# Tables of angles moved beside the projections' batches; columns moved by three engines with a store for each kind

## The reference

```python
q = (x @ Wq).reshape(B, T, H, DK)          # B, T, D = 8, 512, 128; H, DK, M = 8, 64, 8
k = (x @ Wk).reshape(B, T, H, DK)
v = (x @ Wv).reshape(B, T, H, DV)
beta = sigmoid((x @ Wbeta).reshape(B, T, H, M))
tg = sigmoid((x @ Wtg).reshape(B, T, H, M))
angles = pos[:, None, None, None] * omega_scale[None, :, :, None] * inv_freq
cos, sin = jnp.cos(angles), jnp.sin(angles)      # for each time, head, mode and pair: 32 pairs
qr = l2norm(rotary(q, cos, sin)) * scale
kr = l2norm(rotary(k, cos, sin))
g = jnp.log(jnp.clip(tg * rho, 1e-06))
# a scan over time with a state for each mode, batch and head: it takes qr, kr, v, g, beta;
# its outputs are weighted by softmax(mode_logits), gated, multiplied by Wo, and go to the experts
```

## Time and profile before

| | us |
|---|---|
| median of 3 runs | 4490.09 |
| lowest, highest | 4484.92, 4506.94 |
| profiled execution | 4485.37 |
| its span, first to last instruction | 4483.6 |
| project, to the start of tables (15.0 to 276.4) | 261.4 |
| tables with its barrier (276.4 to 391.4) | 115.0 |
| recurrence and experts | 4092.2 |

### The profile page before, as it was taken

How to read it: one execution, slowest core, us unless ns; L and a number is a source line. 1 busy time by engine, 2 the same in 40 slices (tenths; PEclk the granted TensorE clock), 3 DMA queues, 4 the chain that set the end, 5 groups by cost and what they waited for, 6 DMA issues and landing times. The chain is left out here.

```text
span 4483.6 us, 194752 instructions
## 1 busy us (share of the span) xinstructions
PE 3845.0 (86%) x86225; PEld 3102.0 (69%) x86225; DVE 3612.9 (81%) x6975; ACT 2886.8 (64%) x9736; POOL 377.9 (8%) x220
## 2 busy tenths in 40 slices
PE   5511799899999998999899999999998999979999
PEld 2201677777777777777777777777777777756666
DVE  5663988888988888888888888888988888825665
ACT  5752577677766776767677666776766767644443
POOL 1130000000000000000000000000100000000000
PEclk8755899999999999999999999999999999989999
DMA  4667222322232223222322322232223222121110
GB/s 118 173 166 164 60 60 56 91 58 56 56 93 56 63 62 89 60 56 67 82 56 56 80 69 56 56 92 56 56 56 93 56 56 62 50 60 37 34 34 8
DMA packets 319915, 314.47 MB, mean 70 GB/s; under 512 B 139864, under 2 KB 252384, under 8 KB 314976
## 3 DMA queue, kind: packets, MB, share of 16 engines
q1 hardware_dynamic: 319072, 302.00, 26.6%
HBM read 232.70 MB, written 69.21 MB: 67 GB/s over the span
## 5 line engine op out<-in xcount | busy, mean ns | idle before, releaser
L911 DVE TENSOR_TENSOR run_XL<-run_XL,run_EL 128x30 f32<-128x30 f32 (+14 forms) x1920 | 637.6, 332 | 66.0
L910 DVE TENSOR_TENSOR run_EL<-run_AL,run_XL 128x30 f32<-128x30 f32 (+14 forms) x1920 | 637.1, 332 | 66.0
L978 POOL TENSOR_TENSOR run_DB<-run_DB,run_below 128x1024 f32<-128x1024 f32 x128 | 305.0, 2383 | 3310.7 <-DVE run_KP L895 1747.0
L1045 PE MATMUL run_SP<-run_KP 64*32 64x128 f32 x8192 | 552.9, 275 | 30.0 <-DVE run_KP L895 21.7
L871 DVE TENSOR_TENSOR run_SC<-run_SP,run_DB 128x512 f32<-128x512 f32 x512 | 341.2, 686 | 266.9 <-PE run_SP L1049 261.4
L794 ACT ACTIVATE run_DB<-run_DB,run_col 128x64 f32<-128x64 f32 x2048 | 548.0, 351 | 4.7 <-POOL run_DB L978 1.0
L801 ACT ACTIVATE run_KD<-run_PR,run_col 128x64 f32<-128x64 f32 x2048 | 480.3, 328 | 18.4 <-PE run_PR L1064 10.2
L854 ACT COPY run_S<-run_KS 128x256 f32<-128x256 f32 x448 | 166.7, 372 | 504.4 <-PE run_KS L1111 502.4
L1045 PEld LDWEIGHTS run_SP<-run_KP 64*32 64x32 f32 x8192 | 412.6, 107 | 99.2 <-issue 74.2
L807 ACT ACTIVATE run_R<-run_KS,run_col 128x64 f32<-128x64 f32 x1792 | 415.1, 324 | 65.5 <-PE run_KS L1072 65.3
L1007 PE MATMUL run_PR<-ident,run_win 128*64 128x128 f32 x4096 | 285.2, 282 | 169.5 <-DMA run_win<-KQ_s 153.8
(11 more groups left out here) (204 smaller groups left out, 7630.6 us busy)
## 6 DMA issues: line engine op xcount, KB each, us to landing
run_DB<-G_s SPq DMA_DIRECT2D x512, 128.0 KB, 3.0
run_EG<-EG_s SPq DMA_DIRECT2D x128, 512.0 KB, 6.9
run_tab<-TAB_s SPq DMA_DIRECT2D x128, 256.0 KB, 11.8
KQ_s<-proj_win SPq DMA_DIRECT2D x32, 768.0 KB, 7.7
run_win<-KQ_s SPq DMA_DIRECT2D x64, 384.0 KB, 3.2
TAB_s<-tab_tab SPq DMA_DIRECT2D x128, 128.0 KB, 2.4
run_V<-V_s SPq DMA_DIRECT2D x128, 128.0 KB, 3.1
V_s<-proj_vv SPq DMA_DIRECT2D x64, 128.0 KB, 3.2
```

Of the source, the lines that this page charges most:

```text
L910: v.link(dve.tensor_tensor(e, bcast(AL[:, r + 1:, r], 2, done), bcast(XL[:, r, 0:done], 1, rows), ALU.mult))
L911: less = dve.tensor_tensor(XL[:, r + 1:, 0:done], XL[:, r + 1:, 0:done], e, ALU.subtract)
L1045: pe.matmul(out[64 * e:64 * e + C, p].rearrange("p (z u) i -> p z (u i)", z=2), KP[f, key, p, t0:t1], KP[f, kq, p, t0:t0 + SPAN], start=Tr ...
```

## The change

The block `tables` is gone. Its work on a head's tables stands in `project`, head h beside batch h (there are eight of each). On DVE it is cut into four pieces, `angles(b, i)`, one ahead of each tile's sums. On ACT `swing` (the sines) stands at the head of `end(b)`, and `weigh` (the weights) at the next `after(b, 0)`. The buffers `ang` and `turns` are single now. On SP `put_tables(b - 1)` with its 16 stores comes behind the V_s of batch b, and the last head's behind the last KQ_s.

A new block `columns` makes only the 48 copies: ACT the first kind, DVE the second, POOL the third, 16 each, and SP stores each kind when it is there. `cols` has the kind outermost now, so that a store's contiguous piece in DRAM is 32 floats (128 B), where that of the single store was 96 floats (384 B).

```diff
+        ang, turns = sb("ang", [128, 2, T]), sb("turns", [128, 2, T])
+        tab = sb("tab", [128, 2, 4, 2, T])
+        freq = col[:, 1:2]
...
+                def put_tables(h):
+                    sp.wait_ge(tab_done, 3 * (h + 1))
+                    for e in range(2):
+                        for q in range(2):
+                            at = 64 * e + 32 * q
+                            for k in range(4):
+                                sp.dma_start(TAB_s[h, k, e, :, q::2, :], tab[at:at + 32, h % 2, k]).then_inc(put_t[h % 2], 16)
+
                 for b in range(3):
                     load(b)
+                sp.dma_start(pos[:, :], c_pos).then_inc(l_pos, 16)
+                sp.dma_start(col[:, :], c_col).then_inc(l_pos, 16)
...
+                    if b:
+                        put_tables(b - 1)
                 late(B - 1)
+                put_tables(H - 1)
                 for u in range(2):
                     sp.wait_ge(put_x[u], 16 * (B // 2))
                     sp.wait_ge(put_v[u], 16 * 2 * NT * (B // 2))
+                    sp.wait_ge(put_t[u], 16 * 16 * (H // 2))
...
+                def swing(h):
+                    u = h % 2
+                    act.wait_ge(reduced, h + 1)
+                    if h >= 2:
+                        act.wait_ge(put_t[u], 16 * 16 * (h // 2))
+                    act.activation(tab[:, u, 1], ang[:, :], ACT.Sin).then_inc(tab_done, 1)
+                    act.activation(turns[:, :], ang[:, :], ACT.Abs).then_inc(swung, 1)
+                    act.wait_ge(swung, 2 * h + 1)
+                    act.activation(tab[:, u, 0], turns[:, :], ACT.Sin, scale=-1.0, bias=col[:, 0:1]).then_inc(swung, 1)
+
+                def weigh(h):
+                    u = h % 2
+                    act.wait_ge(swung, 2 * h + 2)
+                    act.wait_ge(tab_done, 3 * h + 1)
+                    for j in range(2):
+                        last = act.activation(tab[:, u, 2, j], tab[:, u, 0, j], ACT.Copy, scale=w_part[:, h, j:j + 1])
+                    last.then_inc(tab_done, 1)
+                    for j in range(2):
+                        last = act.activation(tab[:, u, 3, j], tab[:, u, 1, j], ACT.Copy, scale=w_part[:, h, j:j + 1])
+                    last.then_inc(tab_done, 1)
+
                 def after(b, i):
 
+                    if i == 0:
+                        weigh(b)
                     if i == 1:
                         act.wait_ge(decay_in, b + 1)
                         act.activation(z[:, b % 2, :, 0:HM], ez[:, b % 2, :, 0:HM], ACT.Ln).then_inc(logs_out, 1)
@@ -371,6 +416,7 @@
 
                 def end(b):
 
+                    swing(b)
                     if b + 2 < B:
                         act.wait_ge(std_in, b + 3)
                         act.activation(std[:, b % 2], std[:, b % 2], ACT.Sqrt).then_inc(std_out, 1)
...
+                def angles(h, i):
+
+                    a, r = (t[:, :, :].rearrange("p a t -> p (a t)") for t in (ang, turns))
+                    if i == 0:
+                        if h == 0:
+                            dve.wait_ge(l_pos, 32)
+                        else:
+                            dve.wait_ge(swung, 2 * h)
+                            dve.wait_ge(tab_done, 3 * (h - 1) + 1)
+                        for j in range(2):
+                            v(dve.tensor_scalar(ang[:, j], pos[:, :], om_part[:, h, j:j + 1], freq, ALU.mult, ALU.mult))
+                        v.wait()
+                    elif i == 1:
+                        v.link(dve.tensor_scalar(r, a, 1.0 / TWO_PI, ROUND, ALU.mult, ALU.add))
+                        v.link(dve.tensor_scalar(r, r, ROUND, None, ALU.subtract))
+                    elif i == 2:
+                        for part in (CW1, CW2):
+                            v.link(dve.scalar_tensor_tensor(out=a, in0=r, scalar=-part, in1=a, op0=ALU.mult, op1=ALU.add))
+                    else:
+                        v.link(dve.scalar_tensor_tensor(out=a, in0=r, scalar=-CW3, in1=a, op0=ALU.mult, op1=ALU.add))
+                        dve.tensor_scalar(a, a, PI, -PI, ALU.min, ALU.max).then_inc(reduced, 1)
+
                 def tile(b, i):
 
+                    angles(b, i)
                     n = NT * b + i
                     dve.wait_ge(freed_q, 2 * n + 2)
                     dve.tensor_reduce(ssq[:, b % 2, 0, i, :], sqq[:, n % 2, 0, :].rearrange("p (h d) -> p h d", h=H), AX_X, ALU.add).then_inc(summed, 1)
...
-def tables(nc, sems, fresh, c_pos, c_col, om_part, w_part, raw, COL_s, TAB_s):
+def columns(nc, sems, fresh, raw, COL_s):
 
     with ExitStack() as ctx:
...
-        cols = sb("cols", [128, NSEQ, 3, PAIRS, SUPER])
...
+        cols = ctx.enter_context(nc.sbuf_tensor("tab_cols", [128, 3, NSEQ, PAIRS, SUPER], F32))
+        moved, put_c = sems[0:3], sems[3]
+
+        def move(copy, done, arr):
+            for c2 in range(2):
+                for e in range(2):
+                    for p in range(PAIRS):
+                        src = raw[64 * c2:64 * c2 + 64, arr, :, 2 * p + e::M].rearrange(
+                            "t (b i) h -> t h b i", i=NT)
+                        dst = cols[64 * e:64 * e + 64, arr, :, p, c2::2].rearrange(
+                            "t (h b) i -> t h b i", b=B)
+                        copy(dst, src).then_inc(done, 1)
 
         with nc.Block() as block:
             @block.sync
             def _(sp):
-                sp.dma_start(pos[:, :], c_pos).then_inc(loaded, 16)
-                sp.dma_start(col[:, :], c_col).then_inc(loaded, 16)
-                    if h == 2:
-                        sp.wait_ge(moved_a, 2 * 3 * PAIRS)
-                        sp.wait_ge(moved_p, 2 * 3 * PAIRS)
-                        sp.dma_start(COL_s.rearrange("h b p k a c -> p (h b) (k a c)"),
-                                     cols[:, :, :, :, :].rearrange("p n k a c -> p n (k a c)")).then_inc(put_c, 16)
-                for u in range(2):
-                    sp.wait_ge(put[u], 16 * 16 * (H // 2))
-                sp.wait_ge(put_c, 16)
+                for arr in range(3):
+                    sp.wait_ge(moved[arr], 4 * PAIRS)
+                    sp.dma_start(COL_s.rearrange("h b p k a c -> p k (h b) (a c)")[:, arr],
+                                 cols[:, arr].rearrange("p n a c -> p n (a c)")).then_inc(put_c, 16)
+                sp.wait_ge(put_c, 48)
+
+            @block.scalar
+            def _(act):
+                move(act.copy, moved[0], 0)
 
...
+                move(dve.tensor_copy, moved[1], 1)
 
             @block.gpsimd
             def _(pool):
-                for arr in range(3):
-                    move(pool.tensor_copy, moved_p, arr, 1)
+                move(pool.tensor_copy, moved[2], 2)
```

More of the change, by code:

```diff
@@ L95, in keep @@
             return whole.enter_context(nc.sbuf_tensor(name, shape, F32))
-        sems = [nc.alloc_semaphore(f"phase_{i}") for i in range(44)]
+        sems = [nc.alloc_semaphore(f"phase_{i}") for i in range(48)]
         first = sems[0].num
-        assert [s.num for s in sems] == list(range(first, first + 44))
+        assert [s.num for s in sems] == list(range(first, first + 48))
         def fresh():
-            nc.all_engine_barrier(sems_to_clear=range(first, first + 44))
+            nc.all_engine_barrier(sems_to_clear=range(first, first + 48))
         ident = keep("ident", [128, 128])
@@ L175, in prepare, with project @@
         fresh()
-        project(nc, sems, fresh, x, wq, wk, wv, wbt, rho, tri, ones_c, ident, XN_s, raw, KQ_s, V_s, G_s, EG_s)
-        tables(nc, sems, fresh, c_pos, c_col, om_part, w_part, raw, COL_s, TAB_s)
-def project(nc, sems, fresh, x, wq, wk, wv, wbt, rho, tri, ones_c, ident, XN_s, raw, KQ_s, V_s, G_s, EG_s):
+        project(nc, sems, fresh, x, wq, wk, wv, wbt, rho, tri, ones_c, c_pos, c_col, om_part, w_part, ident, XN_s, raw, KQ_s, V_s, G_s, EG_s, TAB_s)
+        columns(nc, sems, fresh, raw, COL_s)
+def project(nc, sems, fresh, x, wq, wk, wv, wbt, rho, tri, ones_c, c_pos, c_col, om_part, w_part, ident, XN_s, raw, KQ_s, V_s, G_s, EG_s, TAB_s):
+    assert B == H
     with ExitStack() as ctx:
@@ L202, in project @@
         gt, gt2, egt = sb("gt", [HM, T]), sb("gt2", [HM, T]), sb("egt", [HM, T])
+        pos, col = sb("pos", [128, T]), sb("col", [128, 4])
+        ang, turns = sb("ang", [128, 2, T]), sb("turns", [128, 2, T])
+        tab = sb("tab", [128, 2, 4, 2, T])
+        freq = col[:, 1:2]
         QB, KB = [ps(f"q{i}", [128, 512]) for i in range(2)], [ps(f"k{i}", [128, 512]) for i in range(2)]
@@ L559, in _ @@
             @block.vector
             def _(dve):
[L561 to L566, removed]
-                    for j in range(2):
-                        v(dve.tensor_scalar(ang[:, u, j], pos[:, :], om_part[:, h, j:j + 1], freq, ALU.mult, ALU.mult))
-                    v.wait()
-                    a, r = (t[:, u].rearrange("p a t -> p (a t)") for t in (ang, turns))
-                    v.link(dve.tensor_scalar(r, a, 1.0 / TWO_PI, ROUND, ALU.mult, ALU.add))
```

(4 more changed lines are left out.)

51 lines of the change are left out of this document (3 added, 48 removed).

## The result

The changed kernel takes 4493.41 us (median of 20 runs, 4487.59 to 4507.17), the kernel before 4482.84 (20 runs, 4475.26 to 4506.94). The ratio is 1.0021, with a 95% interval of 1.0011 to 1.0031: 0.2% slower, or 10.6 us by the medians. I had said 4500 in a range of 4478 to 4526, and a sum of +11.6. Of the 6.6 us between 4500 and 4493.4 most is the kernel before: I had added the sum to 4485 to 4490, and its 20 runs have a median of 4482.8.

A forecast was written before the change was run, and what follows sets the result against it. Project and tables were taken as bound by waits between DVE and ACT, DMA stores and barriers, not by a full engine. -115.0 + 65.7 + 6 + 21 + 33.9 = +11.6 gave 4497 to 4502, stated as 4500 us; range 4478 to 4526.

The forecast's parts named there:

- Swing, 4.5 a cycle in the turn: ACT in project, passing from one batch to the next: sines, absolute value and a table load, uncovered, add 4.5 us a cycle.
- The angles, 6.45 a cycle: DVE in project: the first piece is hidden in idle time, pieces 1 to 3 count in full, 6.45 us a cycle.
- Weigh for nothing: ACT in project, between tiles 0 and 1: 2.6 us of weights cost nothing, covered by 5.03 us of later slack.
- SP fits: SP's queue in project: with 16 more stores it needs 35.3 us in a cycle of 39.3, 4 us to spare.
- the first rival: SP's queue becomes the bound at 1.23 us a store: 44 us a cycle, sum +57, 4545 us; chance 0.08.
- First cycle, +6: Project's first cycle: angles partly hidden by DVE's waits; the rest, swing and one table load add 6 us.
- End of project, +21: From batch 7's first product to the next block: +21 us, 11 from head 6's tables and 9 from head 7's.
- Columns, 33.9: The new block columns: three stores one after the other at 14 ns per 128 B piece, with landing and barrier, +33.9 us.
- The second rival: Columns' stores: 128 B pieces cost what 384 B ones do; stage 48.3 us, sum +26, 4514 us; chance 0.12.
- The third rival: Project: ACT's 5.03 us of idle hides swing, cycle grows by 6.45 only; with cheaper stores -26, 4461 us; chance 0.08.
- The fourth: Rival on ACT in project: each table load also stops ACT for a 1.38 us drain; +23, 4513 us; chance 0.02.
- the ring: Project's cycle from batch to batch: DVE and ACT wait for each other in turn, 28.3 us before, 39.3 forecast.

The follow-up runs named there:

- the first experiment: Changed kernel, but from head 2 on swing works on one column instead of 1024 and has no sine: 4468.32 us in its one run.
- the one version where it can be told apart: Changed kernel with angles at tile 0's head, 8 table stores a head, one column store, swing ahead of raw's exponentials for heads 1 to 7: 4458.56 us, ratio to before 0.9941.

## Why the prediction was right

Each step by its own measure.

- *Swing, 4.5 a cycle in the turn:* 4.49 in the row, and 4.2 with three tiny operations in its place.
- *The angles, 6.45 a cycle:* the pieces take 2.1, 2.5 and 1.9, so 6.5, but the cycle grew by 10.1 to 11.0, 10.45 in the mean, and not by 10.95. The rest is in DVE's groups by shape over the same six batches, of before and then of after:

```profile
L466 DVE TENSOR_TENSOR proj_win<-proj_qk,proj_ssq 128x512 f32<-128x512 f32 x48 | 33.4, 754 | 0.0
```

```profile
L535 DVE TENSOR_TENSOR proj_win<-proj_qk,proj_ssq 128x512 f32<-128x512 f32 x48 | 29.9, 683 | 0.0
```

The products for `win` became 3.5 cheaper in six cycles, 0.6 a cycle. Before, the first four of each cycle, beside POOL's halves in all but one, took 2.48 to 3.70 and the last four 2.49; now all fours take 2.49, and the first of the new pieces has POOL beside it, 1.10 and 0.99 an operation instead of 0.69. I had charged the pieces for POOL and not credited those behind them. Six cycles cost 62.7 where I had 65.7. That 39.3 was the forecast and 39.33 is what five cycles show is partly luck: my 28.3 was a mean that held the short last cycle (26.0), the others had been 28.8 in the mean, and with 10.95 they would have come to 39.7. The last one, 36.1, isn't in the 39 to 40 that I gave for all six.
- *Weigh for nothing:* ACT's idle before L413 is 9.58, so the cover wasn't used up. Right.
- *SP fits:* 0.64 a store, 5.1 us of wait left a cycle where I had 4. Right; the first rival (1.23 a store) falls, but the experiments show how near it was: at 34 a cycle SP is what holds every faster version.
- *First cycle, +6:* 52.63 - 27.04 = 25.6 against 18.3, +7.3. It varies by itself: 24.3 with one column store, whose project is the same, and 25.4 in the changed kernel once more.
- *End of project, +21:* 366.96 - 285.18 = 81.8 against 61.1, +20.7. My own working came to 82.9, which is +21.8 and not the 21 of the sum. Its 2.2 for egt wasn't there: KQ_s of batch 6 starts 26.0 behind batch 7's first product, where I had 27.6.
- *Columns, 33.9:* 33.3. The price of a piece of 128 B was the largest unknown. From the first store to the next block are 24.2, less landing and barrier (3.0 in my sum) 21.2, so 21.2 x 16/24576 = 13.8 ns a piece, where I had 14. The DMA queue in 370 to 406 gives the engines' own time:

```profile
q1 hardware_dynamic: 24768, 3.18, 54.7%
```

36 x 0.547 x 16/24768 = 12.7 ns. The second rival (23.4 ns) falls, and the 10.9 ns of my other estimate lie below both. The copies came out otherwise than I had them, POOL's at 0.75 instead of 0.99 and DVE's at 0.76 instead of at most 0.57, and it made no difference.
- *The third rival*, a hidden swing, falls with the first experiment. As a change of the program it gained nothing in the one version where it can be told apart.
- *The fourth*, a drain behind each table load: L374's load starts at 161.83 and the sine at 163.12, 1.29 later, so none.

Sum of the stages: 62.7 + 7.3 + 20.7 + 33.3 - 115.0 = 9.0. The errors were -3.0, +1.3, -0.3 and -0.6: the largest, the products behind the pieces, is partly hidden by the first cycle's. The sum rests on the mechanism, stage by stage; that it lies within 1 us of the 10.6 of the runs is luck, as the unchanged part varies by more.

Three things that I gave as tests came out otherwise. Recurrence and experts were to stay within 3 us of 4092: both profiles of the changed kernel have over 4102, and among all thirteen only four lie within 3 us. The distance of batches 6 and 7 is 36.1. And the DMA share under the columns' stores is 0.86 (376.2 to 399), not near 1.

## What to carry to other kernels

Work moved beside other work costs by where in the ring it stands, not by how idle its engine is: DVE and ACT were both about 60% busy, and the same angles cost 6 to 7 us a cycle ahead of what ACT waits for and nothing in the wait itself. Before moving more into a stage, add up the in-order queue that issues its transfers; here it was the next floor, 5 us below, and two engines' savings together gained no more than one's. Splitting a store so that it may start earlier must be set against the pieces that it cuts smaller.

## What was not expected of the hardware

Half as many stores of twice the size saved a fifth of SP's time, not half (10.25 to 8.2 us for 2 MB), at a DMA share of 0.95. Three engines that copy [64, 256] pieces at once take 0.57 (ACT), 0.75 (POOL) and 0.76 us (DVE) each. And the same recurrence took 4086 to 4106 us from one profile to the next.
